# Two fused layers on one core: the depthwise convolution moved from VectorE into the projection's matmuls

## The reference

```
xn = layernorm(x)
x  = x + mamba(xn) + moe(xn)            # layer 0
xn = layernorm(x)
x  = x + window_attention(xn) + ffn(xn) # layer 1

def mamba(h):                           # I = 256 channels, N = 16 states, K = 4 taps
    proj = h @ in_proj_w.T;  hs, gate = proj[..., :I], proj[..., I:]
    x = conv(hs over time, conv_w, padding (1, 2), one filter a channel) + conv_b
    u = silu(x)
    dt, Bm, Cm = three rmsnorms of u @ x_proj_w.T
    dt = softplus(dt @ dt_proj_w.T + dt_proj_b);  A = -exp(A_log)
    h_t = exp(dt_t * A) * h_(t-1) + dt_t * u_t * Bm_t      # scan over time, for each state
    y = sum over n of h_t[n] * Cm_t[n] + u * D
    return (y * silu(gate)) @ out_proj_w.T
```

## Time and profile before

| | |
|---|---|
| three timed runs | 1117.99 us median (1116.78 to 1119.48) |
| the profiled execution | 1115.84 us |
| its span (first to last instruction) | 1114.1 us |
| TensorE busy | 861.4 us, 77%, mean granted clock 0.925 |
| VectorE busy | 810.0 us, 73% |
| ScalarE busy | 679.8 us, 61% |
| GpSimd busy | 386.2 us, 35% |
| all DMA | 121.14 MB, 109 GB/s in the mean |

### The profile page before, as it was taken

The page is one execution under the profiler, slowest core; times in us unless marked ns, Lnnn a source line. Parts: engine busy times, 40 slices in busy tenths (PEclk is TensorE's granted clock), DMA queues, the critical chain, the costliest instruction groups (busy, mean ns, idle before and its releaser), DMA issues.

```text
span 1114.1 us, 13822 instructions
## 1 busy us (share of the span) xinstructions
PE 861.4 (77%) x4346; PEld 477.5 (43%) x4346; DVE 810.0 (73%) x1010; ACT 679.8 (61%) x2045; POOL 386.2 (35%) x228
## 2 busy tenths in 40 slices
PE   3553879886697779777977797788878886897893
PEld 2412667663343444334434443343335333443532
DVE  7764444677978897889788968897889788974120
ACT  2132556665577657766776667666756684685680
POOL 3175122213632263226322632254225422641000
PEclk9556999998999999999998989999989899999995
DMA  8164779963331433244324332443234333430001
GB/s 295 39 212 120 228 230 287 264 192 76 82 97 58 123 86 97 57 119 91 97 59 115 93 85 70 105 102 89 71 93 102 80 77 105 102 88 11 19 1 30
DMA packets 85304, 121.14 MB, mean 109 GB/s; under 512 B 8560, under 2 KB 43760, under 8 KB 85104
## 3 DMA queue, kind: packets, MB, share of 16 engines
q1 hardware_dynamic: 78944, 113.45, 36.6%
q0 software_dynamic: 6288, 6.82, 2.7%
HBM read 105.82 MB, written 12.32 MB: 106 GB/s over the span
## 4 chain that ended last, share of the span: by engine, by line
PE 37%; DVE 26%; issue 11%; POOL 11%; ACT 10%; DMA 3%; SPq 1%; DVEq 0%; POOLq 0%; ACTq 0%
PE y_bank L1189 11%; DVE hst L733 10%; POOL hc L1100 4%; PE more L1287 4%; DVE dBu L725 4%; POOL xs_d L1068 3%; POOL x_res L1084 3%; PE work_l L1273 2%; PE work L1273 2%; ACT qbd L976 2%; PE work L1202 2%; ACT dA L917 2%; DVE dc L810 2%; DVE nmax L847 1%; DMA hst<-in_hidden 1%
## 5 line engine op out<-in xcount | busy, mean ns | idle before, releaser
L1100 POOL TENSOR_TENSOR hc<-hst,bcr 128x1024 f32<-128x1024 f32 x102 | 244.3, 2395 | 530.6 <-DVE dBu L725 488.0
L1189 PE MATMUL y_bank<-hc,pk 128*128 128x512 f32 x512 | 269.8, 653 | 83.1 <-POOL hc L1100 66.0
L733 DVE TENSOR_TENSOR_SCAN hst<-dA,dBu 128x1024 f32<-128x1024 f32 x128 | 291.5, 2278 | 3.4 <-issue 2.9
L725 DVE TENSOR_TENSOR dBu<-dtu,bcr 128x1024 f32<-128x1024 f32 x128 | 175.7, 1373 | 12.9 <-DVE hst L733 0.5
L917 ACT ACTIVATE dA<-dt,neg_a 128x511 f32<-128x511 f32 x256 | 171.6, 726 | 17.7 <-DVE hst L733 14.4
L1189 PEld LDWEIGHTS y_bank<-hc,pk 128*128 128x128 f32 x512 | 94.7, 201 | 186.2 <-POOL hc L1100 81.5
L1011 ACT COPY pT<-more 96x512 f32<-96x512 f32 x128 | 74.4, 581 | 100.0 <-PE more L1287 98.3
L1287 PE MATMUL more<-pk,pexp 128*96 128x128 f32 x512 | 102.6, 291 | 10.9 <-ACT pexp L1001 10.4
L1287 PEld LDWEIGHTS more<-pk,pexp 128*96 128x96 f32 x512 | 61.3, 128 | 84.7 <-issue 58.6
L1001 ACT ACTIVATE pexp<-work,nmax 128x96 f32<-128x96 f32 x256 | 83.2, 338 | 15.9 <-DVE nmax L847 15.8
L1001 ACT ACTIVATE pexp<-work_l,nmax 128x96 f32<-128x96 f32 x256 | 83.1, 338 | 1.2 <-DVE nmax L847 1.2
(11 more groups left out here) (303 smaller groups left out, 1475.7 us busy)
## 6 DMA issues: line engine op xcount, KB each, us to landing
bcr<-bc_d SPq DMA_DIRECT2D x128, 512.0 KB
qbd<-in_wx SPq DMA_DIRECT2D x8, 578.0 KB, 4.2
o_all<-in_wx SPq DMA_DIRECT2D x8, 578.0 KB
pT<-in_wx SPq DMA_DIRECT2D x8, 578.0 KB
kT<-in_wx SPq DMA_DIRECT2D x8, 578.0 KB, 5.1
vw<-in_wx SPq DMA_DIRECT2D x8, 578.0 KB, 5.2
xs_d<-rbuf POOLq DMA_DIRECT2D x1, 2560.0 KB, 9.8
hst<-in_hidden SPq DMA_DIRECT2D x8, 256.0 KB, 4.9
```

Source lines behind the costliest of these rows:

```text
L725: v.tensor_tensor(dBu[:], dtu[par], bcr[n % RING][:, 0:1, :].to_broadcast([P, NH, L]), ALU.mult).then_inc(s_dBu, 1)
L733: v.tensor_tensor_scan(hst[n % 2][:].rearrange("p h t -> p (h t)"), dA[n % 2][:].rearrange("p h t -> p (h t)"), dBu[:].rearrange("p h t -> ...
L1100: g_.tensor_tensor(hc[n % 2][:], hst[n % 2][:], bcr[n % RING][:, 1:2, :].to_broadcast([P, NH, L]), ALU.mult).then_inc(s_hc, 1)
L1189: last = t.matmul(y_bank[h][:], ident, hc[n % 2][:, h, :], start=False, stop=(n == N - 1))
```

## The change

The convolution over time of a projection is a sum of four projections of shifted input, with the weights in_proj[:, c] * conv_w[c, k]. VectorE makes these weights once at the start: `conv_row`, the conv weights on every partition, times 0.5 times `in_proj`, 4 x 256 columns, in place. The bias, halved, is split into three bf16 rows (`conv_rows`). For a half, TensorE then adds up in `bank0` one bf16 product (bias rows with ones) and four fp32 products of `xnT` shifted by 0 to 3 columns; `xnT` has a zero margin for it. ScalarE takes tanh of the bank into SBUF (`th`, the memory of `z[0]`), and VectorE makes u = (tanh + 1) * bank in the new units u0, u1, which free the bank. The units conv1 to conv3, th0 and th1 and the tile `hs` are gone, and GpSimd makes `hc` of steps 2 and 3 (except for sequence 0).

In the tables hs0 moves from slot 1 to 0, hs1 from 2 to 3 (behind u0), zg0 from 3 to 4, zg1 from 5 to 6 (behind sg0), sg0 from 4 to 6, sg1 from 6 to 7, u0 is in slot 3, u1 in 4 (were 7 and 8), dtT goes from 15 to 16, the third FFN part from 22 to 21 and to another PSUM bank, `attnT` from 6 to 7. `STEP_AT` gives the slots of the scan steps as a list; they are the same slots as before.

```diff
...
-                      ("wq", H), ("wk", H), ("wv", H), ("wo", H), ("conv_w", NH * KC), ("conv_b", NH),
+                      ("wq", H), ("wk", H), ("wv", H), ("wo", H), ("conv_row", KC * I), ("conv_b", I),
...
-FFN_AT = {12: 0, 17: 1, 22: 2}
-PRE_AT = {0: ["xnT"], 1: ["hs0"], 2: ["hs1"], 3: ["zg0"], 4: ["conv1", "sg0"], 5: ["conv2", "zg1"], 6: ["conv3", "sg1"], 8: ["th1"], 9: ["xdbl"], 10: ["ss"], 12: ["xdr"], 13: ["bc"], 15: ["dtT"], 18: ["dtp0"], 19: ["drl0", "dtp1"], 21: ["drl1"], 22: ["de"], 23: ["dw"], 24: ["dln"], 25: ["dt"], 26: ["dtu"], 27: ["start"], 7: ["th0"]}
-LAYER1_AT = {0: ["out"], 1: ["x1"], 2: ["ln_a"], 3: ["ln_b"], 4: ["q", "k"], 5: ["v0", "v1"], 6: ["v2", "v3"], 27: ["rden"]}
-FINISH_AT = {0: ["rdT"], 5: ["avg"], 6: ["attnT"], 7: ["fin"], 8: ["y_out"]}
-CONV_STEPS = (2, 3)
+FFN_AT = {12: 0, 17: 1, 21: 2}
+PRE_AT = {0: ['xnT', 'hs0'], 3: ['u0', 'hs1'], 4: ['zg0', 'u1'], 6: ['sg0', 'zg1'], 7: ['sg1'], 9: ['xdbl'], 10: ['ss'], 12: ['xdr'], 13: ['bc'], 16: ['dtT'], 18: ['dtp0'], 19: ['drl0', 'dtp1'], 21: ['drl1'], 22: ['de'], 23: ['dw'], 24: ['dln'], 25: ['dt'], 26: ['dtu'], 27: ['start']}
+LAYER1_AT = {0: ['out'], 1: ['x1'], 2: ['ln_a'], 3: ['ln_b'], 4: ['q', 'k'], 5: ['v0', 'v1'], 6: ['v2', 'v3'], 27: ['rden']}
+FINISH_AT = {0: ['rdT'], 5: ['avg'], 7: ['fin', 'attnT'], 8: ['y_out']}
 O_LAG = 3
 EDGE = [("attn", "y_end"), ("finish", "rdT"), ("pre", "xnT"), ("attn", "gated"), ("attn", "out")]
+STEP_AT = (0, 1, 3, 5, 7, 8, 10, 12, 14, 15, 17, 19, 21, 22, 24, 26)
...
-        n = -(-4 * slot // 7)
-        n = n if 7 * n // 4 == slot and n < N else None
+        n = STEP_AT.index(slot) if slot in STEP_AT else None
...
-           "oL": 0, **{f"gate{k}": (1, 0, 1)[k] for k in range(HC)}, **{f"up{k}": 2 for k in range(HC)}}
+           "oL": 0, **{f"gate{k}": (1, 0, 0)[k] for k in range(HC)}, **{f"up{k}": 2 for k in range(HC)}}
...
-        half_c = sb("half_c", [P, NH * (KC + 1)])
+        conv_rows = sb("conv_rows", [96, I], BF16)
+        conv_part = sb("conv_part", [P, I], BF16)
...
-        xnT = sb("xnT", [P, L])
-        hs = sb("hs", [P, NH, L + KC])
+        xnT = sb("xnT", [P, L + KC - 1])
...
+        th = z[0]
...
-            v.memset(hs[:], 0.0).then_inc(s_const, 1)
+            v.memset(xnT[:], 0.0).then_inc(s_const, 1)
...
-            a = PACK["conv_w"][0]
-            v.tensor_scalar(half_c[:], pk[:, a:a + NH * (KC + 1)], 0.5, None, ALU.mult).then_inc(s_const, 1)
+            w_k = pc("conv_row").rearrange("p (k i) -> p k i", k=KC)
+            v.scalar_tensor_tensor(w_k, w_k, 0.5, pc("in_proj")[:, 0:I].unsqueeze(1).to_broadcast([P, KC, I]),
+                                   ALU.mult, ALU.mult).then_inc(s_const, 1)
+            rest = dc[:, 0, 0:I]
+            v.memset(conv_rows[:], 0.0).then_inc(s_cbias, 1)
+            v.tensor_scalar(rest, pc("conv_b"), 0.5, None, ALU.mult).then_inc(s_cbias, 1)
+            for k in range(3):
+                q = slice(32 * k, 32 * k + 1)
+                dve.wait_ge(s_cbias, 2 + 3 * k)
+                v.tensor_copy(conv_rows[q, :], rest[q, :]).then_inc(s_cbias, 1)
+                if k < 2:
+                    v.tensor_copy(conv_part[:], rest).then_inc(s_cbias, 1)
+                    dve.wait_ge(s_cbias, 4 + 3 * k)
+                    v.tensor_tensor(rest, rest, conv_part[:], ALU.subtract).then_inc(s_cbias, 1)
...
-                if (b == 0 and n < DVE_C) or n in CONV_STEPS:
+                if (b == 0 and n < DVE_C):
...
-            def conv(k, b):
-
-                tap = (1, 0, 2, 3)[k]
-                for h in range(NH):
-                    if k == 1:
-                        dve.wait_ge(s_tap, b * NH + h + 1)
-                        done0(dve, b, f"hs{h}")
-                    else:
-                        dve.wait_ge(s_conv, b * NH * (KC - 1) + (k - 2) * NH + h + 1)
-                    v.scalar_tensor_tensor(z[k % 2][:, h, :], hs[:, h, tap:tap + L],
-                                           half_c[:, h * KC + tap:h * KC + tap + 1], z[(k - 1) % 2][:, h, :],
-                                           ALU.mult, ALU.add).then_inc(s_conv, 1)
-
             def pre(name, b, par):
-                if name.startswith("conv"):
-                    conv(int(name[4:]), b)
+                if name in ("u0", "u1"):
+                    h = int(name[1:])
+                    before(dve, s_ys, (b - 1) * (N + 1) + 1)
+                    dve.wait_ge(s_th, b * NH + h + 1)
+                    v.scalar_tensor_tensor(u[:, h, :], th[:, h, :], 1.0, bank0[:],
+                                           ALU.add, ALU.mult).then_inc(s_free0, 1)
                 elif name in ("sg0", "sg1"):
...
-                elif name in ("th0", "th1"):
-                    h = int(name[2:])
-                    before(dve, s_ys, (b - 1) * (N + 1) + 1)
-                    full0(dve, b, name)
-                    v.scalar_tensor_tensor(u[:, h, :], bank0[:], 1.0, z[1][:, h, :],
                                            ALU.add, ALU.mult).then_inc(s_free0, 1)
...
-                    s.copy(xnT[:], bank0[:]).then_inc(s_free0, 1)
+                    s.copy(xnT[:, 1:1 + L], bank0[:]).then_inc(s_free0, 1)
                 elif name in ("hs0", "hs1"):
                     h = int(name[2:])
                     full0(act, b, name)
-                    before(act, s_conv, b * NH * (KC - 1))
-                    s.activation(z[0][:, h, :], bank0[:], ACT.Identity, bias=half_c[:, NH * KC + h:NH * KC + h + 1],
-                                 scale=half_c[:, h * KC + 1:h * KC + 2]).then_inc(s_tap, 1)
-                    s.copy(hs[:, h, 1:1 + L], bank0[:]).then_inc(s_free0, 1)
+                    s.activation(th[:, h, :], bank0[:], ACT.Tanh).then_inc(s_th, 1)
                 elif name in ("zg0", "zg1"):
...
-                elif name in ("th0", "th1"):
-                    h = int(name[2:])
-                    take0(act, b, name)
-                    act.wait_ge(s_conv, b * NH * (KC - 1) + (KC - 2) * NH + h + 1)
...
-                elif name in ("hs0", "hs1", "zg0", "zg1"):
-                    k = ("hs0", "hs1", "zg0", "zg1").index(name)
+                elif name in ("hs0", "hs1"):
+                    q = slice(int(name[2:]) * P, int(name[2:]) * P + P)
+                    if b == 0:
+                        pe.wait_ge(s_cbias, 9)
                     take0(pe, b, name)
-                    t.matmul(bank0[:], pc("in_proj")[:, k * P:(k + 1) * P], xnT[:], start=True,
+                    t.matmul(bank0[:], conv_rows[:, q], onesb[0:96, 0:1].to_broadcast([96, L]), start=True, stop=False)
+                    w_k = pc("conv_row").rearrange("p (k i) -> p k i", k=KC)
+                    for k in range(KC):
+                        last = t.matmul(bank0[:], w_k[:, k, q], xnT[:, k:k + L], start=False, stop=(k == KC - 1))
+                    last.then_inc(s_full0, 1)
+                elif name in ("zg0", "zg1"):
+                    k = NH + int(name[2:])
+                    take0(pe, b, name)
+                    t.matmul(bank0[:], pc("in_proj")[:, k * P:(k + 1) * P], xnT[:, 1:1 + L], start=True,
                              stop=True).then_inc(s_full0, 1)
                 elif name == "xdbl":
                     take0(pe, b, name)
+                    done0(pe, b, "hs1")
...
-        "conv_w": cols(a["L0_attn_conv_w"].reshape(I, KC)), "conv_b": cols(a["L0_attn_conv_b"].reshape(I, 1)),
+        "conv_row": spread(a["L0_attn_conv_w"].reshape(I, KC).T), "conv_b": spread(a["L0_attn_conv_b"]),
...
```

More of the change, by code:

```diff
@@ L161 @@
 EARLY_AT = early()
-L0_USES = [n for lane, n, k in PLAN if lane == "pre" and n in ("xnT", "hs0", "hs1", "zg0", "zg1", "th0", "th1",
+L0_USES = [n for lane, n, k in PLAN if lane == "pre" and n in ("xnT", "hs0", "hs1", "zg0", "zg1",
                                                                 "xdbl", "dtT", "dtp0", "dtp1")]
@@ L181 @@
 PEXP_N = G * RG - O_LAG
-assert L0_N == 11 and len(L1_AT) == len(L1_TURN) == 49
+assert L0_N == 9 and len(L1_AT) == len(L1_TURN) == 49
 def l1_before(b, key, bank=None):
@@ L381, in program @@
         s_moe = sem("expert_rows_in")
-        s_conv = sem("conv_steps")
-        s_tap = sem("first_tap_ready")
+        s_th = sem("u_tanh_ready")
+        s_cbias = sem("conv_bias_steps")
         s_tg = sem("gate_tanh_ready")
@@ L772, in pre @@
                     v.scalar_tensor_tensor(sg[par][:, h, :], tg[:, h, :], 1.0, bank0[:],
-                                           ALU.add, ALU.mult).then_inc(s_free0, 1)
-                elif name in ("th0", "th1"):
-                    h = int(name[2:])
-                    before(dve, s_ys, (b - 1) * (N + 1) + 1)
-                    full0(dve, b, name)
-                    v.scalar_tensor_tensor(u[:, h, :], bank0[:], 1.0, z[1][:, h, :],
                                            ALU.add, ALU.mult).then_inc(s_free0, 1)
@@ L815, in pre @@
                     dve.wait_ge(s_dt, b + 1)
-                    done0(dve, b, "th1")
+                    done0(dve, b, "hs1")
```

(9 more changed lines are left out.)

## The result

| | before | changed kernel |
|---|---|---|
| timed runs beside each other, median | 1117.72 us (1116.78 to 1119.48, 4 runs) | 1111.76 us (1109.39 to 1112.10, 4 runs) |
| the profiled execution | 1115.84 us | 1112.1 us |
| its span | 1114.1 us | 1110.3 us |
| mean granted clock of TensorE | 0.925 | 0.936 |

The ratio is 0.9938, with a 95% interval of 0.9924 to 0.9952: 6 us faster. The forecast was 1107, its range 1093 to 1121.

What follows compares the result with a forecast made beforehand. VectorE and TensorE were both near full, neither at its limit, so lateness in the queues decided. -13.6 (turns 1 to 6) - 0.5 (turn 7) + 3 (start) = -11.1 us on 1115.84, 1104.7; against the runs' median 1107, range 1093 to 1121.

Steps and rivals of the forecast that it cites:

- the front: Scan 0 to scan 6 of a turn, where the convolution lies: forecast at 34.4 us, from 37.8 or 36.1.
- the change hardly touches: The other 75 us of a turn, attention with ten scans, taken as nearly unaffected.
- The walk: Turn 4 followed operation by operation through the engines' queues, 0.1 to 0.2 us per handover: scan 0 to scan 6 in 34.4 us.
- the port: Port pair shared by VectorE and GpSimd: 0 behind steps 2 and 3; as a rival, blocked dBu gives 1147, chance 0.03.
- The front's 13.6 us: Gain in scan 0 to scan 6 over turns 1 to 6: 1.7 us in four, 3.4 in two; bounds 3 and 24.
- The start: Before the first scan: larger pack, weight product and bias chain delay constants 5.7 us; cost taken as +3 us.
- the other branch: At the start, TensorE's clock falls, so zg0, zg1 and the gates end at 51.2: +8.8 us.
- Turn 0's zero: In turn 0 hs0 and hs1 lie in the wait for the scatters, zg0 behind, two tanh handovers go: 0.
- The attention part's 0: Third FFN part a slot earlier on a free bank (0, bounds -1 and +1 a turn), dtT a slot later (0).
- The reason given for the front's long turns: TensorE's clock falls ahead of them (0.74 granted) where it was half idle; with the conv there it doesn't.
- The third rival: Clock dips in the attention part go too and the start costs 0: 1.5 us more in six turns; 1095, chance 0.15.
- turn 7: Last turn, without projection: `hc` 2 and 3 leave VectorE in front of a wait for ScalarE, 0.5 us gained.

Runs made afterwards that it cites:

- the attention part's edits: Third FFN part in slot 21 on another bank, dtT in slot 16: alone on the kernel before 1113.62 us; taken back from the changed kernel 1119.58 us.
- the new order: Changed kernel with u0 and hs1 ahead of scan 2, zg0 ahead of q and k, scan 4 a slot earlier: 1105.84 us, ratio 0.9883.

## Why the prediction was right, and where not

The prediction held in sign and in its account of the front, and its 1107 was 4.8 us too fast. On the profiled executions it had -11.1 and got -3.8. The sign is in part luck: the conv's move with its slots measures 1.000 without the attention part's edits, which the prediction put at 0, and only with them 0.9938. What the front gains there is lost again to falls of TensorE's clock in stretches that "the change hardly touches".

**The walk was right to 0.8 us.** It had steps of 9.35 for scan 2 to 3, 6.9 for 3 to 4 and 4.2 for each of the next two. Measured are 9.4, 7.0, 4.4 and 4.3. The one error of size is scan 1 to 2, 6.5 us for the 6.1 of before. The decays did not delay it: they are ready by 595.36, 1.2 us before scan 2. It was the port, a term that the prediction had at 0 behind steps 2 and 3 and did not look for behind step 1. In VectorE's and GpSimd's timelines of turn 4:

```profile
595.60 0.95 DVE L840 TENSOR_SCALAR var<-mv 128x4 f32<-128x4 f32 x1
```

```profile
594.18 2.35 POOL L1089 TENSOR_TENSOR hc<-hst,bcr 128x1024 f32<-128x1024 f32 x1 [1.75 <-PE y_bank L1174]
```

hs0 stands in front of the D product on TensorE, `hc` of step 1 waits 1.75 us for that product, and the tiny `var` operation ends at 596.55, with GpSimd's `hc` (596.53). Before, the same two were, in turn 4:

```profile
593.96 0.50 DVE L843 TENSOR_SCALAR var<-mv 128x4 f32<-128x4 f32 x1
```

```profile
592.10 2.34 POOL L1100 TENSOR_TENSOR hc<-hst,bcr 128x1024 f32<-128x1024 f32 x1 [1.32 <-DVE dBu L725]
```

There too `var` ends with `hc` (594.46 and 594.44), and `hc` starts 7.36 us behind the turn's scan 0, now 7.80. So hs0's place costs 0.45 us a turn over this meeting. With two taps left out hs0 is 1.7 us shorter, `hc` no longer waits for the product with D, and the step is back at 6.06; in the changed kernel `var` ends with `hc`, within 0.02 us, in all five steady turns. The Trainium skill (SBUF — State Buffer, Who interferes with whom) lists `tensor_scalar` among the operations that can take the shared pair of ports, and says that one side then blocks entirely; the equal ends agree with it. That section excepts just these operations from the rule that the prediction drew on, by which an operation with at most one SBUF input doesn't contend. The prediction had looked at the large operations only. For those its 0 holds: `dBu` has a mean of 1380 ns after and 1373 before, and the meeting of the earlier trace rows is as it was (4.29 for 4.15 us).

**The front's 13.6 us were over-sized, and turn 1 had the wrong sign.** Turns 2 to 6 give 8.2 for 11.9 forecast: the walk's error, five times. Turn 1 gives -3.1 for +1.7. In turn 1 VectorE stands 7 us for a DMA, before its `x1r`:

```profile
261.56 0.69 DVE L828 TENSOR_TENSOR x1r<-x_res,work 128x512 f32<-128x512 f32 x1 [7.03 <-DMA x_res<-ys_d,slot_b]
...
273.98 0.69 DVE L769 SCALAR_TENSOR_TENSOR u<-z,work 128x512 f32<-128x512 f32 x1 [6.01 <-ACT z L924]
```

```profile
261.87 0.69 DVE L831 TENSOR_TENSOR x1r<-x_res,work 128x512 f32<-128x512 f32 x1 [6.99 <-DMA x_res<-ys_d,slot_b]
...
270.05 0.68 DVE L772 SCALAR_TENSOR_TENSOR sg<-tg,work 128x512 f32<-128x512 f32 x1
```

The second fence is of before. There hs0, hs1 and zg0 need nothing of VectorE and run in this pause, so the gate waits for nothing. Now hs1 needs u0, which is queued behind the DMA's reader, and the projection starts after the pause; VectorE waits 6.01 us for it, at a granted clock of 0.67 from scan 2 to scan 3. The step that failed is "Turns 1 to 6: 4 x 1.7 + 2 x 3.4": turn 1 was counted as a steady one without a walk.

**The start came as chosen** (+3.8 for +3): the weight product takes 1.22 us, the chain 2.7 (16.78 to 19.49), and the clock stayed up: 1.00 from 32 to 48 us, where before has 0.50 from 32 to 40. The constants are done 7.3 us later than before, where the walk had 5.7. Three of the experiments' traces show the other branch, which the prediction had at +8.8: their first scans (82.4 to 84.5) are 9.1 to 11.2 us behind that of the kernel before.

**Turn 0's zero was wrong, -4.1.** The prediction looked at hs0, hs1 and zg0, and said that two tanh handovers go, at 0. In turn 0 these handovers stood inside the expert tiles. ScalarE's th0 and its reader on VectorE, before:

```profile
125.83 0.61 ACT L940 ACTIVATE work<-z 128x512 f32<-128x512 f32 x1
```

```profile
126.55 0.69 DVE L778 SCALAR_TENSOR_TENSOR u<-work,z 128x512 f32<-128x512 f32 x1 [0.86 <-ACT work L940]
```

They hold up the tile behind them on both engines. Scan 4 to 5 now takes 4.3 us for 5.3, scan 5 to 6 12.6 for 14.2: 2.5 of the 4.1. That the handovers are the cause is read from the order of the queues; it was not tried apart. The kernels with `hc` back, with the old slots and with the FFN part back have 154.9 to 155.3 us here, the kernel before with the attention part's edits 159.2. The other 1.5 us lie before scan 4, where this turn waits for the scatters in either kernel.

**The attention part's 0, with bounds of 1 us a turn, was mis-sized.** Alone these edits give 4.4 us by their medians, and 7.8 on the changed kernel, 1.3 a turn over six. Not their own work but TensorE's clock, behind GpSimd's gathers and at the edges, makes the 7.8. The reason given for the front's long turns was half right: the falls at scan 2 to 3 (0.74 in the earlier trace rows) are gone in all steady turns, as forecast (9.4 us in each, 1.00 granted). But the kernel with `hc` back has the conv on TensorE too, and falls there in three turns, so the added work alone doesn't hold the clock. In scans 8 to 10 the changed kernel has three long falls and before two; still the sums over turns 1 to 6 are equal (86.8 and 86.7 us). The table's +1.3 us are thus not these falls. They are the edits' own work, +2.3 in scan 10 to 11 and -1.7 in scans 12 to 14, and 0.7 in scan 6 to 7, whose cause stays open. The third rival had these dips gone with the conv's move. They are not; what changes their number is the attention part's edits.

**Left open.** What makes the clock fall in one turn and not in the next, with the same order of instructions and the same pause, no run here settles. So why the attention part's edits hold it up isn't known either, only that they do. Whether the new order keeps it up by its cause or by chance is not settled either. That hs1 freed from u0 in turn 1 alone would give the 3 us back was not tried.

The sum by steps: the walk 3.7 us short, turn 1 4.8, start 0.8, turn 7 0.5, the rest of the turns 1.6, less 4.1 in turn 0: 7.3, the distance between -11.1 and -3.8.

## What to carry to other kernels

Work moved to another engine is worth what the late engine's queue makes of it: here the same conv on TensorE gives +15 us in the old slots, -6 in the changed ones and -13 in the new order, each with the attention part's edits, and 0 in the changed slots without them. When one wait goes, look at the next queue before counting it. Walk each turn that differs, not the typical one alone: a pause for a DMA hides a chain only as long as the chain needs nothing of the engine that pauses. Put a cost on small operations beside GpSimd's long ones. And time an edit that is put at nothing apart from the others: here it decided over all of the gain.

## What the runs showed of the hardware that was not expected

- The runs of one kernel differ by 3 to 13 us between themselves (about 10 us and more in five of the twelve kernels beside the one before), and the traces show where such differences can lie: single stretches of 7 to 15 us in which TensorE's granted clock is 0.78 to 0.80 for 0.88 to 1.00, each worth 1.1 to 1.2 us. The same slots had one such fall in five turns in an execution and three in another.
- The same pause of TensorE, 3.48 us, was followed by no fall of the clock, a short one or a long one: the four products behind it took 1.98, 2.4 to 3.7 or 3.78 us.
- A fall at 40 us of the start (0.50 granted for 1.00) made sixteen small products 3.42 us long for 1.91. In the three executions that had such a start the first scan was 5.3 to 7.4 us later than in the changed kernel's.
- An operation of 128x4 elements took 0.95 us beside GpSimd's product of 128x1024, and 0.17 where it met none (turn 1 of the changed kernel).
